# Graph network on one core: rows of adj and h0 through indirect transfers issued by GpSimd

## What is computed

```
# layer 0: neighbours of the same class, averaged
a   = adj * (y @ y.T)
a   = a / max(sum(|a|, axis=1), 1e-12)
x   = layernorm(x + 0.9 * (a @ x) + 0.1 * h0)
# layer 1: the 350 largest of tanh(adj*adj) in each row
sim = tanh(adj * adj) * (adj > 0)
new = the 350 largest of each row of sim, others 0
x   = layernorm(x + relu(new @ (tanh(x @ W_proj + b_proj) @ W_gcn) + b_gcn))
```

## Time and profile before

| | before |
|---|---|
| median of 3 runs | 468.42 us (467.56 to 468.7) |
| span of the profiled execution, first to last instruction | 465.9 us |
| median less that span | 2.5 us |
| PE busy | 438.7 us (94%) |
| DVE busy | 377.9 us (81%) |
| ACT busy | 263.5 us (57%) |
| POOL busy | 161.5 us (35%) |
| moved by the transfers | 108.50 MB, mean 233 GB/s |

### The profile page before, as it was taken

How to read it: one execution, slowest core, us unless ns; L and a number is a source line. 1 busy time by engine, 2 the same in 40 slices (tenths; PEclk the granted TensorE clock), 3 DMA queues, 4 the chain that set the end, 5 groups by cost and what they waited for, 6 DMA issues and landing times.

```text
span 465.9 us, 15131 instructions
## 1 busy us (share of the span) xinstructions
PE 438.7 (94%) x5104; PEld 386.3 (83%) x5104; DVE 377.9 (81%) x1359; ACT 263.5 (57%) x355; POOL 161.5 (35%) x310
## 2 busy tenths in 40 slices
PE   3659999999999999999999999999999999999994
PEld 2448898888888988888888887888888888888883
DVE  5988999999999999999999976675575575575562
ACT  4997998999999999999999934900000000000000
POOL 3022543455444455554445541221211211211222
PEclk9977999999999999999999999999999999999998
DMA  8999999999999999999999200000000000000000
GB/s 262 411 414 420 419 417 417 415 408 411 409 422 420 422 423 420 424 423 412 417 419 422 60 2 1 13 11 17 17 11 17 17 11 17 17 11 17 17 11 23
DMA packets 25518, 108.50 MB, mean 233 GB/s; under 512 B 5097, under 2 KB 15490, under 8 KB 15490
## 3 DMA queue, kind: packets, MB, share of 16 engines
q1 hardware_dynamic: 25490, 108.14, 57.5%
HBM read 105.57 MB, written 2.56 MB: 232 GB/s over the span
## 4 chain that ended last, share of the span: by engine, by line
PE 75%; DVE 10%; ACT 5%; issue 5%; DMA 2%; POOL 2%; POOLq 0%; DVEq 0%; ACTq 0%; SPq 0%
PE acc L521 64%; PE words L471 6%; DVE a_bits L783 3%; DMA a_rows<-in_adj_dram 2%; PE feat_acc L584 2%; PE proj_acc L595 2%; ACT count_out L685 2%; DVE turned L870 2%; PE xnt_acc L576 1%; ACT count_out L678 1%; ACT x_parts L664 1%; POOL xs L438 1%; ACT count_out L754 1%; DVE z_high L921 1%; ACT count_out L746 1%
## 5 line engine op out<-in xcount | busy, mean ns | idle before, releaser
L521 PE MATMUL acc<-x_parts,turned 128*128 128x257 f16 (+1 forms) x1600 | 195.2, 276 | 3.2 <-DVE turned L870 1.0
L678 ACT ACTIVATE count_out<-a_rows,ones 128x2688 bf16<-128x2688 f32 (+1 forms) x80 | 190.2, 2377 | 0.5 <-DMA a_rows<-in_adj_dram 0.2
L521 PEld LDWEIGHTS acc<-x_parts,turned 128*128 128x128 fp8e4 (+1 forms) x1600 | 154.4, 98 | 28.9 <-issue 3.8
L521 PE MATMUL acc<-f_parts,turned 128*128 128x256 f16 (+1 forms) x1560 | 171.6, 273 | 0.8 <-DVE turned L870 0.8
L521 PEld LDWEIGHTS acc<-f_parts,turned 128*128 128x128 fp8e4 (+1 forms) x1560 | 152.0, 98 | 19.3 <-issue 1.3
L783 DVE TENSOR_SCALAR a_bits<-a_rows 128x2688 bf16<-128x2688 f32 (+1 forms) x80 | 116.7, 1459 | 2.7 <-DMA a_rows<-in_adj_dram 2.3
L421 POOL TENSOR_TENSOR var_eps<-mean_var,consts 128x1 f32<-128x1 f32 x80 | 18.6, 232 | 266.1 <-DVE mean_var L1077 139.7
L870 DVE TENSOR_SCALAR turned<-a_words 128x320 uint16 (+1 forms) x305 | 66.9, 233 | 53.2 <-PE acc L521 52.8
L424 POOL TENSOR_TENSOR rstd<-var_eps,consts 128x1 f32<-128x1 f32 x80 | 86.5, 1081 | 6.3
L870 DVE TENSOR_SCALAR turned<-same_class 128x320 uint16<-128x320 uint16 x313 | 71.3, 254 | 0.1
L471 PEld LDWEIGHTS words<-pack,a_bits 128*128 128x128 bf16 (+1 forms) x1600 | 51.3, 97 | 9.7 <-DVE a_bits L783 7.8
(11 more groups left out here) (111 smaller groups left out, 288.3 us busy)
## 6 DMA issues: line engine op xcount, KB each, us to landing
a_rows<-in_adj_dram SPq DMA_DIRECT2D x39, 1344.0 KB, 7.8
a_rows<-in_adj_dram SPq DMA_DIRECT2D x39, 1156.0 KB, 8.3
out_dram<-xn SPq DMA_DIRECT2D x39, 64.0 KB, 1.5
h_rows<-in_L_gnn_h_dram SPq DMA_DIRECT2D x19, 128.0 KB, 8.1
xs<-in_x_dram SPq DMA_DIRECT2D x3, 640.0 KB, 10.0
xs<-in_x_dram SPq DMA_DIRECT2D x1, 512.0 KB, 10.3
y_nat<-in_L_gnn_y_dram SPq DMA_DIRECT2D x1, 304.0 KB, 3.6
a_rows<-in_adj_dram SPq DMA_DIRECT2D x1, 84.0 KB
```

Of the source, the lines that this page charges most:

```text
L521: mm = pe.matmul(acc[par][0:m, 0:cols], bits, parts[:, b, 0:cols], start=first and b == blocks[0], stop=last and b == blocks[-1])
L678: act.activation(count_out[0:m, 0:w], a_rows[par][h][0:m, 0:w], ACT.Relu, bias=ones[0:m, 0:1], scale=-HUGE, accum_out=col).then_inc(s_coun ...
```

## The change

The loads of adj and h0 leave SP. GpSimd issues each as an indirect transfer: for every partition it takes a row number from the table `row_index`, made once by three iotas, and the transfer reads that row of adj (or h0), from the half's first column on. The rows of a block are the same, in the same order. h0 comes one block at a time, into one of four buffers. In step t GpSimd issues the two halves of block t+1 and h0 of block t ahead of its three parts; in step 0 also block 0. The steps of GpSimd are written out, without a loop. Buffers of adj, and what a load waits for, are as before. The core of the diff:

```diff
+        h0_rows = [sb(f"h0_rows{p}", [P, F]) for p in range(4)]
+        row_index = sb("row_index", [P, NB], U32)
...
         @engines.sync
...
-            load_rows(0, 0, 0)
             sp.dma_start(xs[:, 0, :], x[0:P, :]).then_inc(s_in["x0"], 16)
...
-            load_rows(1, 1, 0)
-            load_h0(0, 0, 0, 0, 0)
-            load_h0(1, 1, 0, 0, 1)
...
-            def step(t, par, pair, i, c):
-                if not isinstance(t, int) or t >= 2:
-                    load_rows(t, par, pair)
-                if valid(t - 1) and c >= 4 and par == 0:
-                    load_h0(t - 1, 1, pair - 1, i, c - 1)
-            steps4(sp, step, 4, 5)
...
         @engines.gpsimd
         def _(pool):
+            pool.iota(row_index[:, 0:1], pattern=[[0, 1]], base=0, channel_multiplier=1).then_inc(s_index, 1)
+            pool.iota(row_index[:, 1:FULL], pattern=[[2 * P, (FULL - 1) // 2], [1, 2]], base=P, channel_multiplier=2)\
+                .then_inc(s_index, 1)
+            pool.iota(row_index[:, FULL:NB], pattern=[[0, 1]], base=FULL * P, channel_multiplier=1).then_inc(s_index, 1)
+            pool.wait_ge(s_index, 3)
...
+            def load_rows(t, par):
+                m = rows_of(t)
+                for h in range(2):
+                    if t >= 2:
+                        pool.wait_ge(s_bits, t * 2 - 3 + h)
+                        pool.wait_ge(s_counted, t * 2 - 3 + h)
+                    pool.indirect_dma_start(a_rows[par][h][0:m, 0:HALF[h].stop - HALF[h].start], None, adj,
+                                            bass.IndirectOffsetOnAxis(ap=row_index[0:m, t:t + 1], axis=0),
+                                            element_offset=HALF[h].start).then_inc(s_rows[par][h], 16)
...
+            def load_h0(n):
+                m = rows_of(n)
+                if n >= 4:
+                    pool.wait_ge(s_h0part, n - 3)
+                pool.indirect_dma_start(h0_rows[n % 4][0:m, :], None, h0,
+                                        bass.IndirectOffsetOnAxis(ap=row_index[0:m, n:n + 1], axis=0)).then_inc(s_h0[n % 4], 16)
...
+            def step(t, par):
                 odd = (par + 1) % 2
+                if t == 0:
+                    load_rows(0, 0)
+                if valid(t + 1):
+                    load_rows(t + 1, odd)
+                if valid(t):
+                    load_h0(t)
                 if valid(t - 2):
-                    residual(t - 2, par, i, c - 2)
+                    residual(t - 2, par)
...
-            steps4(pool, step, LAG, LAG + 2)
+            for t in range(NB + LAG):
+                step(t, t % 2)
```

More of the change, by code:

```diff
@@ L24 @@
 U16 = mybir.dt.uint16
+U32 = mybir.dt.uint32
 F8 = mybir.dt.float8e4
@@ L108, in steps @@
             step(t, t % 2, t // 2)
[L110 to L127, removed]
     def valid(b):
@@ L181, in packed_path @@
         same_class = sb("same_class", [P, NB * WORDS], U16)
-        h0_rows = [sb(f"h0_rows{p}", [P, 2, F]) for p in range(2)]
+        h0_rows = [sb(f"h0_rows{p}", [P, F]) for p in range(4)]
+        row_index = sb("row_index", [P, NB], U32)
         h0_part = sb("h0_part", [P, F])
@@ L250, in packed_path @@
         s_rows = [[sem(f"s_rows{p}{h}") for h in range(2)] for p in range(2)]
-        s_h0 = [sem(f"s_h0{p}") for p in range(2)]
+        s_h0 = [sem(f"s_h0{p}") for p in range(4)]
+        s_index = sem("s_index")
         s_bits = sem("s_bits")
@@ L402, in _, with residual @@
                                base=0, pattern=[[-1, P]], channel_multiplier=1).then_inc(s_const, 1)
-            def residual(n, par, i, c):
-                m = rows_of(n)
-                slot, turn = h0_group(i, c)
-                pool.wait_ge(s_h0[slot], turn * 16 + 16)
+            def load_rows(t, par):
[8 more added lines that the diff above has]
+            def load_h0(n):
+                m = rows_of(n)
+                if n >= 4:
+                    pool.wait_ge(s_h0part, n - 3)
+                pool.indirect_dma_start(h0_rows[n % 4][0:m, :], None, h0,
+                                        bass.IndirectOffsetOnAxis(ap=row_index[0:m, n:n + 1], axis=0)).then_inc(s_h0[n % 4], 16)
+            def residual(n, par):
+                m = rows_of(n)
+                pool.wait_ge(s_h0[n % 4], n // 4 * 16 + 16)
                 pool.wait_ge(s_xh, n)
-                pool.tensor_tensor(h0_part[0:m, :], h0_rows[slot][0:m, h0_place(c), :],
+                pool.tensor_tensor(h0_part[0:m, :], h0_rows[n % 4][0:m, :],
                                    alpha[0:m, :].to_broadcast([m, F]), ALU.mult).then_inc(s_h0part, 1)
                 pool.wait_ge(s_h0part, n + 1)
-                if not isinstance(n, int) or n >= 2:
+                if n >= 2:
                     pool.wait_ge(s_z, n - 1)
```

## The result

The changed kernel takes **538.44 us** (median of 3 runs, 535.44 to 541.6) against 468.42: 1.150 times as long, interval 1.143 to 1.157. The forecast was 542.4 in a range of 478 to 635, with 0.94 on slower. The profiled execution is the longest of the three; it spans 539.8 us (before 465.9), so 73.9 us have to be found in it.

The account below looks back on a forecast made before the run. PE, DVE and transfers were taken as full together, PE closing the 6.30 us step. Span 465.9 + 70 for steps + 4 for the start = 539.9; with 2.5 from span to median, 542.4 us, range 478 to 635.

Parts of the forecast that it names:

- The steps: 35 first-layer steps between the casts of blocks 3 and 38: 8.3 us each instead of 6.30, adding 70 us.
- the start: Before the first products: block 0 now waits on POOL for all of x, costing 3.3 to 5.0, taken as 4 us.
- The price of an issue: POOL's time for one indirect issue: 1.78 us, taken from the mean inverse deviation, which runs into DVE's casts.
- POOL's sum: POOL's own work per first-layer step: 3.13 busy, 0.19 waits inside the residual and 5.34 for three issues, 8.66 us.
- The loop: One DVE step start to the next, through POOL's late issue and the first half's transfer: 7.49 to 8.78 us.
- Turns: Rival, chance 0.20: in the first-layer steps each issue stops DVE; steps of 9.3 to 11.64 us, total 619 us.
- the row at 131.92: Time-line sign against DVE being stopped: where DVE's cast came first, POOL waited and DVE lost nothing.
- Cheap issue: Rival, chance 0.20: an issue costs POOL 0.33 us, first-layer steps grow by 0.3 to about 6.6, total 483 us.
- Not slower: Rival, chance 0.05: steps stay within 6.30 for issues up to 0.59 us; a start gain could give about 466.7 us.
- Cut rows: Rival, chance 0.05: adj transfers split into more packets, rate falls to 385 GB/s, steps 6.8 us, total 490 us.
- The clock: Danger priced at nothing: TensorE's clock could fall to 0.50 (1.2 GHz level) in the steps, with PE 75% busy.
- The second stage: The 190 us behind the cast of block 38, which load nothing, were to stay unchanged.

Follow-up runs that it names:

- SP's own late transfers: Against the changed kernel, SP issues the same loads, each only when POOL reaches its head, and POOL issues nothing: 497.38 us, ratio 1.062.
- the early half: Against the changed kernel, the first half of block t+2 is issued behind step t's residual, ahead of the inverse deviation: 541.97 us, ratio 1.156.
- the small loads: Against the changed kernel, SP issues adj and h0 freely; POOL issues three unread indirect loads of 64-byte rows a step: 532.29 us, ratio 1.137.

## Why the prediction was right, point by point

**The total** came within 4 us of the median and 0.8 of the profiled run (541.6), by two errors against each other, and that closeness is luck. The steps were 7 us too long (70 forecast, 63.0 measured), the start 6.5 us too short (4 forecast, 10.5 measured).

**The price of an issue, 1.78 us.** Measured 1.42 to 1.46, with the gap in front 1.70 for POOL (139.7 / 82). The number was near, though its source was another operation, arithmetic and not an issue, which is luck in part; the reason given was right, an instruction that meets the casts. Its two parts are 0.94 alone and, for about half of them, up to a whole cast on top.

**POOL's sum, 8.66.** Measured 7.6 without the waits for moments. The term that was mis-sized is the arithmetic of 3.13 a step, taken over unchanged: it measured 2.28. The inverse deviation fell from 1784 ns to 582. Before, all 26 of them from 100 to 260 us ran beside a cast; now 24 of 27 run clear of any, in the step shown in the gap ahead of it, where DVE waits for rows. The late issue thus gave POOL back 0.85 us, which the forecast had not seen.

**The loop, 7.49 to 8.78.** With h0 taken off POOL it shows at 7.62, inside the bounds and near the lower one. Two of its terms were off against each other: a half lands 8.4 us behind its issue, not 6.61, and the moments end further ahead of the next cast, as DVE waits 1.6 us in front of it. That the two limits lie close together was right; that the step lies between them was not. POOL's sum alone is 7.6 in the changed kernel, the loop 7.62 with h0 by SP, and at 8.10 the step is longer than either, as now one and now the other closes it.

**The start, 4 us, is the term that failed.** The forecast had POOL free of the wait for x at 11.2 us, the first products near 24.7. Measured are 14.1 and 30.59. First, POOL came past its wait for x 2.9 us later than counted (the last large piece of x landed at 12.91). Second, I took the first products as the measure and gave them 4.0 us from both halves of block 0 (20.7) to there. That path takes 6.86 us from the second cast on (23.73 to 30.59), and it had taken 6.85 before (12.81 to 19.66). In the run the products waited for the parts of x (0.68 us behind DVE line 789 in the row above), which ACT's order holds back until block 0's words are copied, as it did before. So a later block 0 moves the conversion of x too, and the whole pipeline shifts with it: block 0's cast by 10.8 us, the products by 10.9, block 3 by 10.5. Moving block 0's loads ahead gave back 7.0 of the 10.5 at block 3. Moving the conversion of x ahead of block 0's words was not tried.

**Turns fell.** DVE is busy 63.89 us in 80, 6.47 a step at 8.10, against 6.22 before: it lost 0.25 us, not 3 to 5. It is mostly POOL that waits when the two meet, as the row at 131.92 had hinted: 40 of 82 issues got longer, and 6 casts of 54 by more than 0.1 us.

**Cheap issue fell**: lateness alone is 0.64 us a step, twice the 0.3 of that rival, and the issue is not cheap. **Not slower** needed an issue of at most 0.59 us; the shortest indirect one seen is 0.86. **Cut rows fell** on the packets, and indirect transfers are not slower in themselves: from 24 to 32 us, where nothing but them is moved, the DMA engines are full at 421 GB/s. In the steps they are not full: 326 GB/s at a share of 0.87 here, and 376 at 0.98 with SP's own late transfers, about the same for the share. The columns are those of the earlier trace rows.

```profile
24.00:32.00 8.00, 4.42 (x36) 2.70 (x37) 6.93 (x15) 6.14 (x8) 1.56 (x1) 1.00 1.00 421
```

**The clock** was 0.98 of the 2.4 GHz level in the steps, and PE, idle a fifth of the time, did not close them. It was 0.92 and 0.93 from 100 to 250 us in the versions with the early half and with the small loads; there, too, PE has little part in the chain (2.8% for the products with the small loads, under 1.7% with the early half). **The second stage** was unchanged, as forecast; it lasts 209 us from block 38's cast on, not 190, which enters no sum.

## What to carry to other kernels

An issue has a price on the engine that makes it, and it stands in that engine's order like arithmetic: count issues times price (here 0.94 to 1.06 us alone, about 1.7 with its gap on the mean beside busy casts) against that engine's free time in a step, before asking what the transfers do. Where two limits lie close, take away one at a time, and read in the chain of waits which one is left. Here the step had lost 1.80 us, and taking away one limit gave back 0.05, which is nothing clear, the other 0.49, since each leaves the other standing. At a pipeline's start, follow the first block through every engine's program order, since what it makes late there is late for everything behind it.

## What was not expected of the hardware

- The price of an indirect issue hardly depends on what it loads: 0.86 us for 16 rows, 1.02 for 128 of 64 bytes, 0.94 for 128 rows of 10 KB with DVE idle. Most have about 0.30 us in front that ends on nothing the profile shows; plain issues by POOL have none (0.1 us in 42).
- Contention with DVE's casts is lopsided in this kernel: an issue that meets one about doubles, while the casts of the two halves take 1.58 and 1.43 us on the mean, against 1.56 and 1.35 before (100 to 320 and 100 to 260 us). An issue that began up to 0.56 us ahead of a cast still ends behind it.
- The same arithmetic on POOL became three times faster (the inverse deviation, 1784 to 582 ns) as it came to run at another moment of DVE's step.
